# First block, LoRA preparation and scale work rearranged in a quantised cross-attention and LoRA feed-forward kernel

## The reference

```python
x = x + xattn(layernorm(x), ctx)          # x (2, 1024, 2048), ctx (2, 2048, 2048)
    # fake_quant(v) = (clip(round(v / s + z), 0, 255) - z) * s, on both operands, then matmul
x = x + ffn(layernorm(x))                 # W (2048, 2048)
    # base = y @ W + bias
    # A_eff[g] = sum_n gate[g, n] lora_A[n],  B_eff[g] likewise, g = 8 groups of 256 tokens
    # out = base + (y A_eff^T) B_eff^T + (y A_s^T) B_s^T       rank 32 each
```

## Time and profile before

| | |
|---|---|
| median of 3 runs | 1089.86 us (1089.62 to 1090.78) |
| the profiled execution | 1092.13 us, of which its span is 1090.5 us |
| PE busy | 1000.6 us, 92% of the span |
| DVE, ACT, POOL busy | 520.9, 313.8, 161.2 us |
| mean PE clock granted | 0.986 |

### The profile page before, as it was taken

How to read it: one execution, slowest core, us unless ns; L and a number is a source line. 1 busy time by engine, 2 the same in 40 slices (tenths; PEclk the granted TensorE clock), 3 DMA queues, 4 the chain that set the end, 5 groups by cost and what they waited for, 6 DMA issues and landing times.

```text
span 1090.5 us, 12123 instructions
## 1 busy us (share of the span) xinstructions
PE 1000.6 (92%) x4727; PEld 467.9 (43%) x4727; DVE 520.9 (48%) x746; ACT 313.8 (29%) x270; POOL 161.2 (15%) x192
## 2 busy tenths in 40 slices
PE   0699599889899998999999999999999999999996
PEld 0265234345354443444444444444454444444442
DVE  6643275977844465456332654777824014005010
ACT  3883741322212123214213565422212012003000
POOL 2001000021101302401510000020102204003100
PEclk9999899899999999999999999999999999999998
DMA  8988491457848416524699955257937016004000
GB/s 368 279 252 356 146 356 71 139 145 141 218 137 285 137 58 226 185 117 160 180 356 223 380 202 194 39 145 139 167 136 244 20 41 220 13 35 154 10 33 34
DMA packets 132455, 183.79 MB, mean 169 GB/s; under 512 B 104384, under 2 KB 104384, under 8 KB 119616
## 3 DMA queue, kind: packets, MB, share of 16 engines
q1 hardware_dynamic: 118784, 126.64, 39.2%
q0 software_dynamic: 12480, 52.44, 13.3%
q10 hardware_dynamic: 1152, 4.19, 1.0%
HBM read 128.72 MB, written 29.36 MB: 145 GB/s over the span
## 4 chain that ended last, share of the span: by engine, by line
PE 56%; DMA 13%; DVE 10%; issue 6%; ACT 5%; POOL 2%; SPq 2%; DVEq 0%; POOLq 0%; ACTq 0%
PE psum L940 13%; PE psum L1074 13%; PE psum L1076 13%; PE psum L1075 13%; DMA stage<-in_w 3%; DMA xn<-in_x 3%; DMA bias_sb<-in_bias 2%; PE psum L1097 2%; POOL x L579 2%; DVE ring L1297 2%; DMA stage<-in_ctx_in 1%; ACT ring L698 1%; ACT x L843 1%; DMA a_scratch<-lhs 1%; DVE x L1350 1%
## 5 line engine op out<-in xcount | busy, mean ns | idle before, releaser
L1074 PE MATMUL psum<-ring,lhs 128*128 128x512 f16 x1024 | 388.1, 379 | 15.7 <-DVE ring L1297 7.0
L1076 PE MATMUL psum<-ring,lhs 128*128 128x512 f16 x1024 | 388.1, 379 | 0.0
L1075 PE MATMUL psum<-ring,lhs 128*128 128x512 f16 x1024 | 388.1, 379 | 0.0
L940 PE MATMUL psum<-ring,lhs 128*128 128x512 bf16 x1024 | 237.1, 388 | 37.1 <-DMA lhs<-hl 32.1
L940 PEld LDWEIGHTS psum<-ring,lhs 128*128 128x128 bf16 x1024 | 101.6, 100 | 165.0 <-issue 42.0
L1074 PEld LDWEIGHTS psum<-ring,lhs 128*128 128x128 f16 x1024 | 100.2, 98 | 139.8 <-issue 11.6
L1076 PEld LDWEIGHTS psum<-ring,lhs 128*128 128x128 f16 x1024 | 100.2, 98 | 120.8
L1075 PEld LDWEIGHTS psum<-ring,lhs 128*128 128x128 f16 x1024 | 100.2, 98 | 119.0
L1350 DVE SCALAR_TENSOR_TENSOR x<-psum,sc,x 128x512 f32<-128x512 f32 (+1 forms) x64 | 45.3, 746 | 183.3 <-PE psum L1086 182.4
L698 ACT ACTIVATE ring<-stage,sc 128x2048 f16<-128x2048 f32 x32 | 63.6, 1999 | 207.9 <-PE psum L1076 158.6
L579 POOL TENSOR_TENSOR x<-x,bias_sb 128x512 f32<-128x512 f32 (+1 forms) x64 | 90.1, 1435 | 177.3 <-DVE xn L1332 96.7
(11 more groups left out here) (129 smaller groups left out, 615.9 us busy)
## 6 DMA issues: line engine op xcount, KB each, us to landing
stage<-in_w SPq DMA_DIRECT2D x38, 1024.0 KB, 6.8
stage<-in_ctx_in SPq DMA_DIRECT2D x32, 1024.0 KB, 6.6
out<-x POOLq DMA_DIRECT2D x64, 256.0 KB, 3.3
x<-in_x POOLq DMA_DIRECT2D x8, 1024.0 KB, 14.4
xn<-in_x POOLq DMA_DIRECT2D x8, 1024.0 KB, 7.3
x<-in_x POOLq DMA_DIRECT2D x4, 2048.0 KB, 15.1
lhs<-in_lora_a SPq DMA_DIRECT2D x4, 1024.0 KB, 6.8
lhs<-in_lora_b SPq DMA_DIRECT2D x4, 1024.0 KB, 11.4
```

What stands on the lines that cost most here:

```text
L940: last = pe.matmul(psum[:, t, :], lhs_q[:, k, t * P:(t + 1) * P], ring_q[:, g, j % 2, u, :], start=(k == 0), stop=False)
L1074: pe.matmul(psum[:, t, :], hi, ring[:, g, 0, u, :], start=(kk == 0), stop=False)
L1075: pe.matmul(psum[:, t, :], hi, ring[:, g, 1, u, :], start=False, stop=False)
L1076: last = pe.matmul(psum[:, t, :], lo, ring[:, g, 0, u, :], start=False, stop=False)
```

## The change

Nothing of the arithmetic changes. In block 0, batch 0:

- POOL issues x tiles 0 to 3, then, behind its waits for DVE's statistics, ctx groups 2 and 3 into the free half of `ring` (`load_head`), x tiles 4 to 7, and the four `lora_a` loads, which SP issued before. SP keeps ctx groups 0 and 1 and all transposes.
- `q_slots` becomes six buffers (two more in `ap_st`); the rows' sums are written to `b_st`, three of the eight sums go to DVE.
- ACT begins with a one-element Sqrt, so that the table load stands ahead of x.
- PE takes only tiles 0 and 1 group by group, then the column sum, then tiles 2 to 7 one by one.
- ctx groups 2 and 3 no longer use `stage`, so that the numbering of its uses shifts by two.

In the LoRA part, the copies have four buffers instead of two, and `b_eff_out` alternates with the long `row_terms`. POOL's first reduction stands behind the four stores of B. DVE's `power_a` moves into block 1, W's maxima are spread over blocks 1 to 3, and gates 2 and 3 move from block 1 to block 2.

```diff
+        halves = [v[:, h * D // 2:(h + 1) * D // 2] for v in (hl32, xn[:, :], ap_st[:, :]) for h in range(2)]
+        QS = len(halves)
-        a_part = [ap_st[:, c * D // 2:(c + 1) * D // 2] for c in range(2)]
-        b_part = [hl32[:, c * D // 2:(c + 1) * D // 2] for c in range(2)]
+        a_part = halves[4:6] + halves[0:2]
+        b_part = a_part
+        SUMS = TILES - 3
...
@@ SP
             load_ctx(0, 0, [0, 1])
-            turn_q(0)
-            turn_q(1)
-            load_ctx(0, 0, [2])
...
+            for t in range(6):
+                turn_q(t)
+            load_ctx(0, 1, [0])
             turn_q(6)
             turn_q(7)
-            load_ctx(0, 1, [0, 1])
+            load_ctx(0, 1, [1])
...
@@ POOL
-            for t in range(TILES):
-                pool.dma_start(x2[:, t, :], x_tile[0, t]).then_inc(x_in[t], 16)
+            def load_head(g):
+                pool.dma_start(head_buf(g), ctx_v[0, 0, g].rearrange("p (h u) n -> p h (u n)", h=2)).then_inc(head_in[g - 2], 16)
+            load_x(range(4))
...
             root_pair(0)
+            load_head(2)
+            load_x([4])
+            load_head(3)
+            load_x([5])
+            root_pair(1)
+            load_x([6, 7])
+            for c in range(NBLK):
+                pool.dma_start(la_slot(c), lora_a[c]).then_inc(la_in[c], 16)
...
@@ ACT
+                    relu_rows(5)
+                    sum_rows(0)
+                    sum_rows(1)
+                    relu_rows(6)
+                    relu_rows(7)
+                    for t in range(2, SUMS):
+                        sum_rows(t)
                     act.wait_ge(rows_ready, b + 1)
+                    for c in range(NBLK):
+                        for k in range(c * KC, (c + 1) * KC):
+                            a_eff_out(k)
+                        ctx_block(b, 1, [c])
                     for n in range(8):
+                        row_term(n, 1, NBLK)
                         b_eff_out(n)
-                    row_terms(1, NBLK)
...
@@ PE, first_block
                 for g in range(NG):
                     ring_ready(0, 0, g)
-                    for t in range(half):
+                    for t in range(2):
...
                 column_sum(0, 0)
-                for t in range(half, TILES):
+                pe.wait_ge(pats, 6)
+                for t in range(2, TILES):
...
@@ DVE, evict_and_convert and after
+                if b == 0 and j == 1:
+                    power_a()
+                if b == 0 and j == 2:
+                    max_of_first_w(1)
...
-                if j == 1:
+                if j == 2:
                     gate_low(b, 2)
                     gate_low(b, 3)
```

More of the change, by code:

```diff
@@ L135, in build @@
         (SP0, SP1, SP2, SP3, IS1, IS2, S12, SPARE, D2S, KD, T0, T1, MX_A, MX_W, MX_B, PW_A, PW_W, PW_B,
-         SA, ISA, SS, RSTD, ROUND_BACK, VEPS, ROOT, D1) = [col(i) for i in range(26)]
+         SA, ISA, SS, RSTD, ROUND_BACK, VEPS, ROOT, D1, ONE) = [col(i) for i in range(27)]
         RC = sc[:, 30:38]
@@ L199, in build @@
         sh_again = sem("sh_again")
-        ag_dram = [sem("ag_dram0"), sem("ag_dram1")]
+        ag_dram = [sem(f"ag_dram{n}") for n in range(NBLK)]
         ag_in = sem("ag_in")
@@ L212, in build @@
         be_out = sem("be_out")
-        bg_dram = [sem("bg_dram0"), sem("bg_dram1")]
+        bg_dram = [sem(f"bg_dram{n}") for n in range(NBLK)]
         scales = sem("scales")
@@ L341, in load_ctx @@
                         sp.wait_ge(act_conv, act1(b, j, g) - 1)
+                    if b == 0 and j == 1 and g < 2:
+                        sp.wait_ge(act_conv, g + 1)
                     elif b:
@@ L355, in load_gates @@
                 if b == 0:
-                    for n in range(2):
-                        sp.wait_ge(ag_dram[n], 16 * (NBLK // 2))
+                    for n in range(NBLK):
+                        sp.wait_ge(ag_dram[n], 16)
                     sp.wait_ge(be_full, 6)
@@ L403, in _ @@
             load_first_w(1)
-            load_ctx(0, 3, range(NG))
+            load_ctx(0, 3, [0, 1])
             load_first_w(2)
+            load_ctx(0, 3, [2])
             load_first_w(3)
+            load_ctx(0, 3, [3])
             def turn_next(b, t):
@@ L485, in _ @@
                     sp.wait_ge(a_dram[n], 16 * (b + 1) * (GPB // 2))
-                    if b == 0:
-                        sp.wait_ge(bg_dram[n], 16 * (NBLK // 2))
+                if b == 0:
+                    for n in range(NBLK):
+                        sp.wait_ge(bg_dram[n], 16)
                 load_a(b, 0)
@@ L514, in _, with load_x @@
         def _(pool):
[L516 to L519 removed]
+            def load_x(tiles):
+                for t in tiles:
+                    pool.dma_start(x2[:, t, :], x_tile[0, t]).then_inc(x_in[t], 16)
+            def load_head(g):
+                pool.dma_start(head_buf(g), ctx_v[0, 0, g].rearrange("p (h u) n -> p h (u n)", h=2)).then_inc(head_in[g - 2], 16)
             def root_pair(p):
@@ L837, in column, with row_term @@
                     act.activation(col_parts[:, n % 2, :], psum[:, CB, :], ACT.Copy, scale=D1).then_inc(col_hi, 1)
+                def row_term(t, first, last):
+                    v = x2[:, t, first * NW:last * NW]
+                    act.activation(v, v, ACT.Identity, bias=RC[:, t:t + 1]).then_inc(with_row, 1)
                 def row_terms(first, last):
                     for t in range(TILES):
-                        v = x2[:, t, first * NW:last * NW]
-                        act.activation(v, v, ACT.Identity, bias=RC[:, t:t + 1]).then_inc(with_row, 1)
+                        row_term(t, first, last)
                 if b == 0:
@@ L945, in ring_ready @@
             def ring_ready(b, j, g):
-                pe.wait_ge(converted, grp1(b, j, g) + 1)
+                if b == 0 and j == 0 and g >= 2:
+                    pe.wait_ge(head_conv, g - 1)
+                else:
+                    pe.wait_ge(converted, grp1(b, j, g) + 1)
             def column_sum(b, j):
@@ L1178, in _ @@
             then(dve.memset(ROUND_BACK, -(ROUND + CENTRE)))
+            then(dve.memset(ONE, 1.0))
             then(dve.reciprocal(IS1, S1))
@@ L1270, in ctx_group, with head_group @@
                     add_group(b, j, g)
+            def head_group(g):
+                dve.wait_ge(head_act, g - 1)
+                dve.tensor_scalar(ring_q[:, g, 0, :, :], ring_i[:, g, 0, :, :], 255.0, -CENTRE,
+                                  ALU.min, ALU.add).then_inc(head_conv, 1)
             def add_group(b, j, g):
@@ L1545, in _ @@
             round1(7)
+            for t in range(SUMS, TILES):
+                sum_rows(t)
             LAP = 6 * LNB + SCALE_STEPS
@@ L1554, in _ @@
                         peaks_a()
-                        power_a()
                         peaks_b()
@@ L1559, in _ @@
                     if b == 0 and j == 2:
-                        for g in range(1, NG):
-                            max_of_first_w(g)
-                        all_of_w(0)
-                        power_b()
+                        max_of_first_w(2)
                 j = NBLK - 1
                 column_low(b, j)
+                if b == 0:
+                    max_of_first_w(3)
+                    all_of_w(0)
+                    power_b()
                 early_stats2(b, 0)
```

194 lines of the change are left out of this document (89 added, 105 removed).

## The result

The changed kernel takes 1083.64 us (1079.1 to 1085.55, 8 runs), the kernel before on the same chip 1090.72: ratio 0.993, interval 0.9916 to 0.9945, faster by 7.1 us. Its profiled execution took 1083.35 us, of which the span is 1081.5, where it was 1090.5.

The account below looks back on a forecast made before the run. PE, busy 92% of 1090.5 us, was taken as the bound, with only idle and slow time to gain. Terms +0.1, -2.9, -4.7, -7.2, +4.0, +1 gave -9.7: 1082.4 profiled, 1080 median; own range 1076 to 1084, wide range 1065 to 1089.

Parts of the forecast that it names:

- rival C: LoRA part: alternation costs more, ctx lands at 104.8, column sum at 123, `power_a` loses its cover; 1085 us, chance 0.13.
- Queue 0 dry at 44.3 and PE at 46.5: Start: queue 0 runs dry after 16 transfers at 44.3; PE starts at 46.5, 14.4 later than before.
- one-for-one turn of small and large packets: Start: beside busy queue 0, queue 1's transpose gets one small packet for each of up to 8 KB.
- rival A: Start not starved: transposes get several packets per queue 0 packet, PE starts at 32; 1066 us, chance 0.17.
- Rival B: Start: queue 0 drains more slowly beside six transposes; at 0.2 MB/us PE starts at 68, 1102 us; chance 0.12.
- seven further groups at 0.216 us: Block 0: seven further groups of four matmuls for tiles 0 and 1, 0.216 us per matmul, done at 54.6.
- my bound: LoRA part: late bound for block 1's last ctx group, 104.8; 17.0 after first `lora_b` load plus 2.7 for later issue.
- start, block 0 and LoRA +0.1: Sum's first term: late start and alternation use up the removed 9.65 us wait; block 1's column sum 119.1 against 118.99.
- one of my two signs of being wrong: The signs: first matmul before 40 or after 55 us, or POOL's reduction ending after 131.
- The waits of 2.9 and 2.7: Blocks 1 and 2: rounding wait and column-sum wait go, with 2 us of slow clock; terms -2.9 and -4.7.
- The wait of 6 us for the transpose: Before phase 2: PE waits 6 us for tile 1's transpose instead of 1.95, and may lose 1 us to slow clock.
- Later stages: "not changed": Behind phase 2's first product: no change in time, so the sum stays at -9.7 us.

Follow-up runs that it names:

- e1: Changed kernel with POOL's four `lora_a` loads issued only after the last inverse root and tile 4's transpose: 1073.68 us, 16.3 less than the kernel before.
- e3: Kernel before with only the four `lora_a` loads moved to POOL's queue, right behind the x tiles: 1101.35 us, 11.4 more than before.
- e9: e1 with 57 extra matmuls on PE ahead of tile 0, their result overwritten: 1065.44 us, 26.1 less than the kernel before.
- e11: Changed kernel with 104 extra matmuls on PE ahead of tile 0: 1081.03 us, 10.5 less than the kernel before; one launch left out.
- e4: Kernel before with the spreading alone (W's maxima over blocks 1 to 3, `power_b` behind the rounding, gates 2 and 3 in block 2): 1083.23 us.
- e5: e4 plus the LoRA part (four buffers, alternation, POOL's reduction after B's stores, `power_a` in block 1), old start kept: 1072.22 us, ratio 0.9833.
- e10: e5 without the alternation, B's eight copies together and the eight long row terms behind them: 1070.87 us, 20.6 less than the kernel before.
- e12: e10 with 29 extra matmuls on PE ahead of tile 0: 1074.77 us, 16.8 less than the kernel before.
- e2: e1 with x tiles 6 and 7 also issued late, after tile 3's transpose: 1084.72 us, 5.3 less than the kernel before.
- e7: e1 with 28 extra matmuls on PE ahead of tile 0: 1075.75 us, 14.8 less than the kernel before.

## Why the prediction was right, and where it wasn't

The forecast was 1080 (own range 1076 to 1084), the runs gave 1083.6. The mechanism of the start and of blocks 1 to 3 was right. Against the profiled time it said -9.7, measured were -8.8; against the median before on the same chip the gain was 7.1. Two errors, 5.3 and 4.2 us, nearly cancel, and that was luck: without the second the time would have been about 1088, outside my own range. 1083.6 is also nearer to rival C's 1085 than to 1080.

- **The start.** Queue 0 dry at 44.3 and PE at 46.5: about 45 and 47.60. The one-for-one turn of small and large packets held. So did the reasons: starved transposes behind queue 0. The rule of the Trainium skill's page DMA: Bandwidth & Descriptors (Queues, rings and completion order), by which several descriptors go for one turn, isn't borne out by these 109 and 109 packets; rival A fell with it. e1 and e3 show that the loads of `lora_a` on queue 0 are the cause. Rival B (slower drain) did not come: queue 0 moved 0.79 MB in those 2 us.
- **From there to the end of block 0: 81.4 predicted, 84.22 measured.** Besides the 1.1 us, the step "seven further groups at 0.216 us" was mis-sized. Tiles 0 and 1 took 9.65 us until the column sum (57.25), not 8.1, for PE ran at the slow pace after 47 us of idle time, which e9 and e11 take away. I took the pace from a stretch of the kernel before in which PE had not stood still that long, and there the slow matmuls were hidden in the waits for tiles 1 to 3.
- **LoRA.** The last ctx group of block 1 was converted at 106.6, 18.7 us behind the first `lora_b` load (87.93), not 15.9; my bound was 19.7. The pairs took 15.7 us (16.0 forecast). So "start, block 0 and LoRA +0.1" was the step that failed in size: +5.4, column sum at 124.43 for 119.1. Of the 5.3 us missing, 2.8 come from the end of block 0 and 2.8 from the load of ctx, whose reason stays open; the pairs give back 0.3. Rival C had 123 and 1085, so this half of it came. Its other half, `power_a` without cover, did not: POOL's reduction had 6.19 us of idle time ahead of it instead of 8.2, and PE had no wait at 136.69. But it began at 131.48, so one of my two signs of being wrong, a reduction that ends after 131, did come; it was only a sign that this stretch ran late.
- **Blocks 1 and 2.** The waits of 2.9 and 2.7 and the slow clock behind the latter went: from the column sum to block 2's first tile 27.8 us (before 30.7), block 2 29.6 (before 34.1). Predicted -2.9 and -4.7, measured -2.9 and -4.5. The second comes from the spreading: e4 alone has 29.6 too. The first doesn't: e4 keeps 30.7 (118.80 to 149.47) with its wait of 2.34, and e5, with the LoRA part, has 27.7 (114.20 to 141.93). With the row terms behind the copies again, e10 has a wait of 1.88 in that place, so it is their new place that removes the wait, as predicted.
- **Phase 2.** DVE reached its statistics at 190.40, 5.4 us earlier, not 10.8; the missing 5.4 are the late column sum from above. The wait of 6 us for the transpose came as 6.28, and the slow clock behind it.
- **Later stages: "not changed", and that was wrong by 4 us.** From phase 2's first product on the changed kernel needed 863.7 us, that of before 867.9: the waits of PE put down to issue fell from 5.6 to 2.4, those for `ring` from 7.0 to 4.8. This offset most of the 5.4. Both are one execution each, and the runs of the changed kernel alone lie 6.5 us apart (1079.1 to 1085.55), so part of the 4 us can be scatter. e9 and e12 show that this part moves by more than that when its start shifts a little, and I can't give a rule for it.

The parts of the sum hid how large they were: I had the LoRA part's gain and the late start cancel, which is what happened, but either is 11 us. About 9 of the start's 11 were four loads on a queue on which nobody waited (e1).

## What to carry to other kernels

In these traces a transpose by DMA that started while another queue streamed large packets got one small packet for each of them (109 and 109 in 2 us), however late the data of those transfers were wanted. So hold back on that queue what isn't needed yet, and look on the list of each engine what stands behind the data you hold back (e1 gained 9 us, e2 lost it again). When PE must wait for the start anyway, extra work can help its first real matmuls: work that reached right up to them had them done in 7.07 us, work that ended 6.4 us before left them at 8.40 (e9, e7). What it does to the whole time has to be measured, since e9 gained 9.8 us by it and e12 lost 3.9. And when a change of three parts moves little, time each part alone: here two of them gained 18 us and the third lost 11.

## What the runs showed of the hardware that I had not expected

- Two transposes of 128x2048 in a 2-byte type took SP 26.9 us beside a busy queue 0, and the next two took it 4.9 us once queue 0 was dry.
- PE's first matmuls of the changed kernel ran at half pace while the granted clock in that stretch reads 1.00:

```profile
48.00:50.00 2.00, 2.00 (x6) 0.57 (x5) 0.00 (x0) 0.00 (x0) 0.00 (x0) 1.00 1.21 248
50.00:52.00 2.00, 2.00 (x6) 0.76 (x5) 0.00 (x0) 0.00 (x0) 0.00 (x0) 1.00 1.13 211
```

  Six matmuls in 2 us is the pace of the earlier trace rows, where the clock reads 0.50. Only e7, in which PE had worked before, shows the lower level in the same place. In these two stretches the record can't be taken at its word, since e9 has eleven matmuls in 2 us at the same reading; the count of matmuls in a stretch must be read instead. The Trainium skill's page TensorE: Matmul & The Clock Gate (Seeing it yourself) says that such clock events of a trace can't be fully trusted; this trace agrees.
